# Attention and routed experts on one core: first score units two tiles later, a lead of four rows, rotation as one product, routing inside the first head, and sums and stores on other engines

## The reference

```
xn = (x - mean) / sqrt(var + 1e-5)                   # over the last axis
q, k, v = split(xn @ w_qkv.T); q, k = rope(q), rope(k)
        # rope(x) = x * cos + concat(-x2, x1) * sin, on the halves x1, x2 of each head
attn = softmax(q @ k.T / 4); s = (attn @ v) @ w_out.T  # for each head
e = argmax(xn @ gate_w.T)                             # one expert for each row
f = (relu(xn @ wg[e])**2 * (xn @ wu[e])) @ wd[e]
out = x + s * silu(f)
```

## Time and profile before

| | us |
|---|---|
| median of 3 runs | 1651.2 (1650.79 to 1651.39) |
| the profiled execution | 1654.93 |
| its span, first to last instruction | 1653.2 |
| PE busy | 1539.2 (93%) |
| DVE busy | 1367.1 (83%) |
| ACT busy | 1189.0 (72%) |
| POOL busy | 141.1 (9%) |

### The profile page before, as it was taken

One profiled execution on the slowest core, in us unless ns is written; L12 is line 12 of the kernel. 1 busy time (PEld: TensorE's weight loads), 2 busy tenths in 40 slices (PEclk: granted clock), 3 DMA queues, 4 the chain that ended last, 5 costly groups with the idle time before them and its releaser, 6 DMA issues.

```text
span 1653.2 us, 29704 instructions
## 1 busy us (share of the span) xinstructions
PE 1539.2 (93%) x9121; PEld 660.2 (40%) x9121; DVE 1367.1 (83%) x1563; ACT 1189.0 (72%) x2381; POOL 141.1 (9%) x160
## 2 busy tenths in 40 slices
PE   6897999989899999999999999999999999999998
PEld 4453333346433333333333333333333333333336
DVE  7678799964599999999999999999999999999705
ACT  4452377855677787787788778778777877877780
POOL 2232322100122100000010000000010000000100
PEclk9998599989899999999999999999999999999999
DMA  5673234425444324222222242222222422222303
GB/s 199 226 193 117 55 78 100 67 48 154 103 78 78 61 42 93 42 42 42 39 40 41 39 90 39 39 41 41 41 42 42 90 39 39 41 40 35 62 4 118
DMA packets 77820, 116.54 MB, mean 70 GB/s; under 512 B 29072, under 2 KB 64272, under 8 KB 70800
## 3 DMA queue, kind: packets, MB, share of 16 engines
q1 hardware_dynamic: 69632, 101.89, 31.9%
q0 software_dynamic: 3072, 8.39, 2.0%
q10 hardware_dynamic: 5072, 5.72, 1.0%
HBM read 75.31 MB, written 39.85 MB: 70 GB/s over the span
## 4 chain that ended last, share of the span: by engine, by line
PE 74%; ACT 17%; DVE 3%; issue 3%; DMA 2%; SPq 1%; ACTq 0%; POOLq 0%; DVEq 0%
PE ps L1114 31%; PE ps L1103 31%; ACT arena L582 16%; PE ps L1035 3%; PE ps L1193 2%; PE ps L1036 1%; PE ps L1094 1%; PE ps L1209 1%; PE ps L1239 1%; DVE arena L692 1%; PE ps L1059 1%; DMA arena<-xs_d 1%; PE ps L1166 1%; PE ps L1046 1%; DMA out<-arena 1%
## 5 line engine op out<-in xcount | busy, mean ns | idle before, releaser
L726 DVE TENSOR_REDUCE arena<-ps 128x1 f32<-128x1024 f32 x992 | 1174.1, 1219 | 127.3 <-PE ps L1094 119.2
L582 ACT ACTIVATE arena<-ps 128x512 f32<-128x512 f32 x2048 | 1059.7, 603 | 275.3 <-PE ps L1103 274.1
L1103 PE MATMUL ps<-qs,ks 50*128 50x512 f32 x2048 | 754.5, 449 | 61.0 <-ACT arena L582 29.5
L1094 PE MATMUL ps<-ks,qs 48*128 48x512 f32 x1984 | 796.3, 474 | 4.3 <-DVE arena L726 2.5
L1103 PEld LDWEIGHTS ps<-qs,ks 50*128 50x128 f32 x2048 | 341.9, 186 | 685.6 <-issue 436.2
L1114 PE MATMUL ps<-arena 128*32 128x512 f32 x4096 | 551.6, 611 | 0.8 <-ACT arena L582 0.8
L1094 PEld LDWEIGHTS ps<-ks,qs 48*128 48x128 f32 x1984 | 331.9, 187 | 48.0 <-DVE arena L726 17.0
L1114 PEld LDWEIGHTS ps<-arena 128*32 128x32 f32 x4096 | 80.9, 108 | 130.3 <-ACT arena L582 113.7
L969 POOL COPY arena<-v_sb 128x256 f32 (+1 forms) x32 | 13.3, 416 | 1108.1 <-ACT arena L574 1090.8
L1035 PE MATMUL ps<-arena 128*128 128x512 f32 x128 | 68.8, 620 | 0.7 <-ACT arena L496 0.7
L692 DVE TENSOR_REDUCE arena<-ps 128x1 f32<-128x1024 f32 x32 | 39.1, 1222 | 23.8 <-PE ps L1059 23.8
(11 more groups left out here) (103 smaller groups left out, 543.0 us busy)
## 6 DMA issues: line engine op xcount, KB each, us to landing
qs<-parts_d SPq DMA_DIRECT2D x186, 128.0 KB
ks<-parts_d SPq DMA_DIRECT2D x186, 128.0 KB
parts_d<-arena SPq DMA_DIRECT2D x64, 256.0 KB, 2.6
xs_d<-arena SPq DMA_DIRECT2D x13, 384.0 KB, 3.4
arena<-xs_d SPq DMA_DIRECT2D x13, 384.0 KB, 3.8
ys_d<-arena SPq DMA_DIRECT2D x13, 384.0 KB, 2.8
onum_d<-arena SPq DMA_DIRECT2D x128, 32.0 KB
out<-arena ACTq DMA_DIRECT2D x16, 256.0 KB, 2.1
```

The costliest lines, as they stand in the source:

```text
L582: nc.scalar.activation(prob[kb % 2][:, c * W:(c + 1) * W], ps[:, bank, :], ACT.Exp, scale=SCALE).then_inc(exp_done[bank], 1)
L726: nc.vector.tensor_reduce(most[head_slot][:, tile, u:u + 1], ps[:, AB + 2 * u:AB + 2 + 2 * u, :], AX.XY, ALU.max).then_inc(a_reduced[u], 1)
L1094: ins = nc.tensor.matmul(ps[:, AB + c, :], qs[head_slot][ABASE:ABASE + KR, tile * P:(tile + 1) * P].bitcast(F32R), ks[head_slot][ABASE:ABA ...
L1103: nc.tensor.matmul(ps[:, bank, :], ks[s][0:KS, kb * P:(kb + 1) * P].bitcast(F32R), qs[s][0:KS, c * W:(c + 1) * W].bitcast(F32R), start=Tru ...
```

## The change

- The eight single units of head 0 move from slots 12 to 19 to slots 14 to 21.
- `rotate` becomes one product of 1024 elements a row, which needs a table `turn` laid out as cos, cos, sin, -sin: GpSimd builds `turn` from `rope` in four copies at the start, and adds the halves of each tile in two additions of 256 elements instead of one of 512.
- AHEAD goes from KB + 5 to KB + 4. `cut_maxima` runs two of its four instructions at a time: k = 0, 1 behind the last reduction of step 11, k = 2, 3 behind the first of step 12.
- `choose` stands behind the reductions of the first of the four lead tiles, and so behind head 0's `cut_maxima`. The three first b-scores stand ahead of the last lead tile; the counts go to bank PVB, and ScalarE copies them out behind its third exponential. `assign` stands in step 1 of head 0.
- `sums_out` goes from ScalarE to VectorE, at the start of the next head's step 0, ahead of its reductions.
- The stores of the result alternate between ScalarE's queue (even blocks) and SP's (odd ones), and the last chunk is multiplied ahead of block 4 instead of block 6.
- The rows of -1 in `ks` are set by GpSimd instead of VectorE at the start; ScalarE's two table loads take their input from a word that VectorE sets. VectorE's loop over the first two pairs is written out.

```diff
-    UNITS = {t: ((t - HB - 4, 0),) for t in range(HB + 4, 2 * HB + 4)}
+    UNITS = {t: ((t - HB - 6, 0),) for t in range(HB + 6, 2 * HB + 6)}
...
-    AHEAD = KB + 5
+    AHEAD = KB + 4
...
+            for n in range(1, B * ENDT, 2):
+                sp.wait_ge(res_ready[n % NR], n // NR + 1)
+                sp.dma_start(out_v[:, 2 * n:2 * n + 2, :], res[n % NR]).then_inc(res_stored[n % NR], 16)
...
-            def sums_out(s, pi):
-
-                act.wait_ge(pv_done[1], past(pi * KB + (s + 1) * NB2))
-                act.wait_ge(spread_in[s], past(pi * 16))
-                act.wait_ge(o_stored[s], past(pi * (16 * QT)))
-                nc.scalar.copy(osb[s], ps[:, PVB, :]).then_inc(o_out[s], 1)
...
-                        if kb == 0 and c == 2 and not first:
-                            sums_out(1 - s, pi - 1 + s)
-
-            exps(0, 0, True)
-            exps(0, 1, False)
-            for pi in range(1, FB):
+                        if isinstance(pi, int) and pi == 0 and s == 0 and kb == 0 and c == 2:
+                            act.wait_ge(counts_done, 1)
+                            nc.scalar.copy(counts, ps[:, PVB, 0:2 * E]).then_inc(counts_out, 1)
...
+            for n in range(0, B * ENDT, 2):
+                act.wait_ge(res_ready[n % NR], n // NR + 1)
+                act.dma_start(out_v[:, 2 * n:2 * n + 2, :], res[n % NR]).then_inc(res_stored[n % NR], 16)
...
-            for i in range(2):
-                nc.vector.memset(ks[i][32:64, :], -1.0).then_inc(first_ones, 1)
+            nc.vector.memset(table_in[:, 0:1], 0.0).then_inc(table_set, 1)
...
-                    dve.wait_ge(rope_done, t - 1)
-                nc.vector.tensor_tensor(u4, q2, tab[:, :, 0:hd].to_broadcast([P, 2 * QK // DH, hd]), ALU.mult)
-                nc.vector.tensor_tensor(b4[:, :, 0, :], q4[:, :, 1, :],
-                                        tab[:, :, 2 * hd:3 * hd].to_broadcast([P, QK // DH, hd]), ALU.mult)
-                nc.vector.tensor_tensor(b4[:, :, 1, :], q4[:, :, 0, :],
-                                        tab[:, :, hd:2 * hd].to_broadcast([P, QK // DH, hd]), ALU.mult).then_inc(rotated, 1)
+                    dve.wait_ge(rope_done, 2 * (t - 1))
+                full = [P, heads, 2, DH]
+                nc.vector.tensor_tensor(rab[t % 2].rearrange("p (h w d) -> p h w d", w=2, d=DH),
+                                        qk_s[t % GT].rearrange("p (h o d) -> p h o d", o=1, d=DH).to_broadcast(full),
+                                        turn[:, t:t + 1, :].rearrange("p o (w d) -> p o w d", w=2).to_broadcast(full),
+                                        ALU.mult).then_inc(rotated, 1)
...
-            choose()
             base[0], count[0] = SETUP_STEPS, 0
             for k in range(CUTS):
                 cut_maxima(k, 0, 0)
             for t in range(KB, AHEAD):
                 for u in range(2):
                     reduce(t, t // KB, t % KB, u)
+                if t == KB:
+                    choose()
...
+            def sums_out(s, pi):
+
+                dve.wait_ge(pv_done[1], past(pi * KB + (s + 1) * NB2))
+                dve.wait_ge(spread_in[s], past(pi * 16))
+                dve.wait_ge(o_stored[s], past(pi * (16 * QT)))
+                nc.vector.tensor_copy(osb[s], ps[:, PVB, :]).then_inc(o_out[s], 1)
...
+                if kb == 0 and not (isinstance(pi, int) and pi == 0 and s == 0):
+                    sums_out(1 - s, pi - 1 + s)
+                if kb == 1 and s == 0 and isinstance(pi, int) and pi == 0:
+                    assign()
...
-                    k = 2 * (ahead - KB) + u + 1
+                    k = 2 * (2 * (ahead - KB) + u + 1)
                     if 0 <= k < CUTS and coming:
                         cut_maxima(k, pi * 2 + (s + 1), 1 - s, s, (pi + 1) * 64)
+                        cut_maxima(k + 1, pi * 2 + (s + 1), 1 - s, s, (pi + 1) * 64)
...
-            assign()
-            with dve.Fori(0, FB) as pi:
+            for pi in range(FB):
...
-                    if n == ENDT - 2:
+                    if n == ENDT // 2:
...
+            pool.wait_ge(consts_ready, 1)
+            for i in range(2):
+                nc.gpsimd.memset(ks[i][32:64, :], -1.0).then_inc(first_ones, 1)
+            pool.wait_ge(first_ones, 2)
+
+            pool.wait_ge(weights_loaded, 16 * NW)
+            hd = DH // 2
+            for lo, src in ((0, 0), (hd, 0), (2 * hd, hd), (3 * hd, 2 * hd)):
+                nc.gpsimd.tensor_copy(turn[:, :, lo:lo + hd], rope[:, :, src:src + hd]).then_inc(turn_ready, 1)
...
-                TT(rq[t % 2], ra[t % 2], rb[t % 2], ALU.add).then_inc(rope_done, 1)
+                turned = rab[t % 2].rearrange("p (h w a d) -> p h w a d", w=2, a=2, d=DH // 2)
+                out = rq[t % 2].rearrange("p (h a d) -> p h a d", a=2, d=DH // 2)
+                for a in range(2):
+                    TT(out[:, :, a, :], turned[:, :, 0, a, :], turned[:, :, 1, 1 - a, :], ALU.add).then_inc(rope_done, 1)
...
+                if t == AHEAD - 1:
+                    pe.wait_ge(loaded[0], 16 * LOADS)
+                    pe.wait_ge(shift_loaded[0], 64)
+                    for c in range(QT - 1):
+                        score(0, 0, 0, c)
                 for c in range(QT):
                     score_a(t, t // KB, t % KB, c)
             pe.wait_ge(own_ready, 1)
-            nc.tensor.matmul(ps[:, 0, 0:E], before_b[:], own_b, start=True, stop=True)
-            nc.tensor.matmul(ps[:, 0, E:2 * E], ones_b[:], own_b, start=True, stop=True).then_inc(counts_done, 1)
+            nc.tensor.matmul(ps[:, PVB, 0:E], before_b[:], own_b, start=True, stop=True)
+            nc.tensor.matmul(ps[:, PVB, E:2 * E], ones_b[:], own_b, start=True, stop=True).then_inc(counts_done, 1)
```

More of the change, by code:

```diff
@@ L92, in layer_kernel @@
         gate = sb("gate", [P, NT, D])
-        rope = sb("rope", [P, NT, 3 * DH // 2])
+        turn = sb("turn", [P, NT, 2 * DH])
         ident = sb("ident", [P, P])
@@ L131, in layer_kernel @@
         tmp = cut([4, NT])
-        ra = [cut([QK]) for _ in range(2)]
-        rb = [cut([QK]) for _ in range(2)]
+        rab = [cut([2 * QK]) for _ in range(2)]
         rq = [cut([QK]) for _ in range(2)]
         logits = cut([NT, E])
+        rope = cut([NT, 3 * DH // 2])
         GROUPS_END = at[0]
@@ L245, in layer_kernel @@
         first_ones = sem("first_ones")
+        turn_ready = sem("turn_ready")
+        table_set = sem("table_set")
         consts_ready = sem("consts_ready")
@@ L466, in _ @@
                 act.dma_start(dst, src).then_inc(first_loaded, 16)
-            for dst, src in ((rope[:], rope_in), (rank[:], rank_in)):
+            for dst, src in ((rope, rope_in), (rank[:], rank_in)):
                 act.dma_start(dst, src).then_inc(weights_loaded, 16)
@@ L536, in _ @@
                 high_part(t)
-            nc.scalar.activation(table_in[32:64, 1:2], ks[0][32:64, 0:1], ACT.Exp, scale=0.0)
-            act.wait_ge(counts_done, 1)
-            nc.scalar.copy(counts, ps[:, 0, 0:2 * E]).then_inc(counts_out, 1)
+            nc.scalar.activation(table_in[:, 2:3], table_in[:, 0:1], ACT.Exp, scale=0.0)
             for i in range(2):
@@ L594, in _ @@
                 for s in range(2):
-                    exps(pi, s, False)
-            sums_out(1, NP - 1)
-            for b in range(B):
-                for i in range(ENDT):
-                    n = b * ENDT + i
-                    act.wait_ge(res_ready[n % NR], n // NR + 1)
-                    act.dma_start(out_v[:, 2 * n:2 * n + 2, :], res[n % NR]).then_inc(res_stored[n % NR], 16)
+                    exps(pi, s)
+            for n in range(0, B * ENDT, 2):
+                act.wait_ge(res_ready[n % NR], n // NR + 1)
+                act.dma_start(out_v[:, 2 * n:2 * n + 2, :], res[n % NR]).then_inc(res_stored[n % NR], 16)
             for i in range(NR):
@@ L860, in _ @@
             pair(NP - 1, True)
+            sums_out(1, NP - 1)
             invert(1, NP)
@@ L1040, in turn_q @@
             def turn_q(t):
[L1042 removed]
+                pe.wait_ge(rope_done, 2 * (t + 1))
                 if t:
```

23 lines of the change are left out of this document (7 added, 16 removed).

## The result

The changed kernel takes 1641.05 us (median of 4 runs, 1638.55 to 1642.82) against 1651.3 for the kernel before (4 runs, 1650.79 to 1651.62): a ratio of 0.9937, with an interval of 0.992 to 0.9954. Run again on two other chips (e0_again, e0_third) it took 1639.18 and 1639.01, and the kernel before 1652.39 and 1652.34. So the gain is 10 to 13 us. The forecast was 10.15, and its closeness to the first median is partly luck: the two profiled executions, from which its terms were read, differ by 16.5.

A forecast was written before the change was run, and what follows sets the result against it. The prediction took a ring over TensorE and ScalarE to bound the steps, with VectorE close. Its terms summed to -10.15 us, 1644.8 on the profiled execution, so a median of 1641.1; 1634 to 1648 held eight in ten.

The forecast's parts named there:

- Unit 0: Tile loop: moving the units two tiles later ends TensorE's wait for ks; -8.0 us, between -4.0 and -8.8.
- rival (2): Tile loop: the loads of ks are no longer in time and unit 0 waits again; 4 us gives 1645; chance 0.08.
- Start: Kernel start: with GpSimd on ks, VectorE's statistics and so TensorE start sooner; -0.65 us, between 0 and -0.7.
- Rival (4): Rotation: GpSimd and VectorE exclude each other, up to +4 us over some 14 tiles, so 1645; chance 0.05.
- Lead of four: First steps: one lead tile less puts the steps ahead by one; -2.3 us, between 0 and -4.1.
- sums_out: Turn of heads: copy leaves ScalarE, -6.8 us, less 1.5 for VectorE's lateness; -5.3, between -6.8 and +4.7.
- reserve of b-score 2: Plain step: VectorE's reduction may be 0.34 us late before the step grows, or 0.14 with the other spacing.
- rival (1): VectorE's side work is hidden whole and cut_maxima in pairs costs nothing, so 1636.6 us; chance 0.14.
- cut_maxima: Steps around 12, each head: pairs make reductions 0.49 us late, 0.15 over the reserve; +4.5 us, between 0 and +10.5.
- rival (3): Turns of heads: VectorE becomes the bound and both latenesses are paid; +10.5 us, 1661.7; chance 0.05.
- Experts: Loads of the experts' rows on SP's queue stand behind a shift that comes later; +0.2 us, once.
- The end: Last blocks: VectorE waits for the last chunk ahead of block 4, delaying block 8; +1.4 us, alternatives +3.0 or -4.2.

The follow-up runs named there:

- e1: Changed kernel with only the eight single units of head 0 put back to slots 12 to 19: 1651.63 us, ratio 1.0005 to the kernel before.
- e4: Changed kernel with GpSimd setting the rows of ks behind its four table copies instead of ahead of them: 1640.25 us, ratio 0.9932 to the kernel before.
- e8: Changed kernel with the rotation as before (three products, one addition, no turn table): 1640.92 us, ratio 0.9932 to the kernel before.
- e7: Changed kernel with lead of five, routing and single cut_maxima as in the kernel before: 1639.11 us, ratio 0.9918 to the kernel before.
- e10: e9 with lead and routing as before the change (five tiles, choose and assign ahead of the steps): 1631.46 us, ratio 0.9875 to the kernel before.
- e9: Changed kernel with cut_maxima spread singly, ks rows set late and the last chunk loaded by two DMAs: 1628.25 us, ratio 0.9857 to the kernel before.
- e3: Changed kernel with cut_maxima spread (k = 0, 1 behind one reduction each, 2 and 3 behind the third): 1638.85 us, ratio 0.9919 to the kernel before.
- e5: Changed kernel with the last chunk multiplied ahead of block 6 again, stores still on two queues: 1639.85 us, ratio 0.9925 to the kernel before.
- e6: Changed kernel with the last chunk's load issued as two DMAs, one for each head: 1634.11 us, ratio 0.9901 to the kernel before.

## Why the prediction was right

- **Unit 0**, -8.0: right in place and size (-8.0; e1 gives 8.1 back). The margin of the loads held, so rival (2) fell.
- **Start**, -0.65: wrong in sign, +0.7 at TensorE's first product and the first tile. The step that failed is "their statistics follow without a gap, with GpSimd on ks: -0.65". The statistics did come 0.96 sooner, but what follows them was held for 1.3 until the memset ended (e4). The table copies, which the forecast let end "long before the first tile is rotated", cost 0.3 more beside the scaling of x (e8). Rival (4) had named such an exclusion for the rotation. The forecast says that no row shows either engine waiting; in the trace of the kernel before there is one such row (50.70, 0.98 instead of 0.70). It arises in one tile of 32 and costs nothing that shows (tiles 22 to 31: 0), the additions taking 0.72. By tile 12 the loss is 0.2.
- **Rotation**, 0: right as a sum, since 0.5 gained in tiles 0 to 12 pays for the table copies (e8); the forecast had neither. One product of 1.23, two additions of 0.72.
- **Lead of four**, -2.3: right in mechanism and sign. The wait of 1.0 put ahead of the last lead tile was 0.18, so step 2 was 4.1 sooner and not 3.0. And the clock did not rise "in the same place": 2.9 more by step 5 in this execution. But about 3 of these 7.0 are not the lead's, as e7 and e10 show: with the old lead and the rest of the change the stretch is already that much shorter than in the one profiled execution of the kernel before, and whether that is the rest of the change or this execution's late clock stays open. By the eleven profiles with four and the two with five, the lead is worth 2.0 to 4.1 up to step 5; e9 against e10 gives 1.4 to 3.2 in all. The -2.3 lies inside both.
- **sums_out**, -5.3: -6.4. The reserve of b-score 2 is there, and no smaller than computed: a copy with 0.61 to the next start costs no step anything. The 0.1 a pair was too careful; of rival (1) this half holds.
- **cut_maxima**, +4.5: +5.1 to 5.3, in step 13 where it was placed, 0.13 and 0.21. The other half of rival (1) fell. So did rival (3): no turn pays its whole lateness.
- **Experts**, +0.2: seen in the wait, not in the time. TensorE waits 4.22 for the experts' rows instead of 3.79, but the pause between the steps around the experts is 81.87 in both. With `mrow` later still it costs 1.1 (e3). The 1.7 in the two steps behind it goes with 6.8 us at half clock instead of 10.2; no step of the forecast had it.
- **The end**, +1.4: +1.1, by the wait named; e5 gives 0.1 to 0.7 of it to the place of the product, and leaves 0.5 open. e6 shows that the load's shape is the cause of the wait. Its end part is 4.2 below the kernel before's, the forecast's own price for a load that is there in time.

The profiled spans fall by 6.4 more than the sum of the forecast: 4.7 of it between tile 31 and step 5 (-7.0 for -2.3), 1.7 in the steps behind the experts, 0.6 in the other steps (-1.2 for -0.6), 0.3 at the end, less 0.9 at the start. The medians fall by only 10.3 to 13.3, since the profiled execution of the kernel before was 3.7 above its median and that of the changed kernel 2.5 below. The forecast's two extremes, 1629 and 1651, are not what its terms give: the favourable ends add up to -24.4, or 1626.8, and the unfavourable ones, with `sums_out` at -5.3, to +4.4, or 1655.6. Its range doesn't rest on them. What was not settled: why the clock returns earlier in one execution than in another. It moves the time by 2 to 5 us with the same code, as much as most of the edits.

## What to carry to other kernels

Where a ring over two engines sets the step, ask of a third engine how late each of its instructions may be, in one step and at one place, not how busy it is: here 0.61 us in one piece was free at one place, and twice 0.33 us lost 0.13 to 0.21 at another. A small instruction alone between two long ones nearly vanished (0.07 of its 0.17 us); two dependent ones in a row cost nearly their whole length (0.33 from 1337.76 to 1338.09). And read how a broadcast load is split before you move its wait about: two loads instead of one were worth about 5 us, the place of the wait 0.1 to 0.7.

## What was not expected of the hardware

- A VectorE instruction on 4 elements a row took 1.10 to 1.69 us instead of 0.17, always until a GpSimd memset of 32 x 2048 ended. The rotation's product, where it falls beside a GpSimd addition, takes 1.50 instead of 1.23, or 0.98 instead of 0.70.
- A load whose slowest dimension is 2 took 8.3 us to its last packet; the same bytes as two loads of 16 rows each, 3.4 from the second issue.
- The same program had mean granted clocks of 0.982 to 0.985 from run to run, with times of 1642.8 and 1637.6 at the two ends; the kernel before 0.975 to 0.981, with times of 1646.8 to 1654.8.
